# An attention program for two batches: written out in place of a loop of two turns

## The chip, the core and the metric

The kernel runs on one core of a Trainium2 chip. The core has five engines that run their own instruction streams side by side and meet at semaphores: TensorE (PE, matmuls and transposes), VectorE (DVE), ScalarE (ACT), GpSimd (POOL) and SyncE (SP, which here only issues DMAs). The metric is the device time in microseconds, the median of several executions.

## The reference

One transformer layer with adaptive layer norm, for two batches of 2048 tokens with 256 features. Attention has two query heads that share one key and one value head of 128; it is causal. The second half is a mixture of eight experts in which every expert is computed for every token and weighted by a thresholded gate.

```python
mod = (silu(c) @ wmod)                       # shifts, scales and gates, per batch
h = layernorm(x) * (1 + ca) + sa
k = rope(h @ Wk.T); v = h @ Wv.T; q = rope(einsum('btd,hkd->bhtk', h, Wq))
w = softmax(causal(q @ k.T * HS**-0.5)); o = w @ v
x = x + ga * (o @ Wo.T)
h = layernorm(x) * (1 + cb) + sb
gate = softmax(h @ Wg + bg); thr = sigmoid(h @ Wt + bt) * 0.125
g = where(gate >= thr, gate - thr, 0); g = g / sum(g)
x = x + gb * sum_e g_e * (gelu(h @ W1[e] + b1[e]) @ W2[e] + b2[e])
```

All in float32; products are made of three matmuls of split operands (hi*hi, hi*lo, lo*hi).

## The kernel before

The program has two blocks with a barrier of all engines between them: attention (up to about 503 us of the profile) and the mixture (the rest).

Attention handles the 4096 tokens as 2 batches of 16 tiles of 128. For each tile there are stages: `norm`, `rstd` and `xn` (layer-norm statistics, reciprocal root, normalized rows; three engines pass small tiles round), `normT` (transposition and modulation), `hT` and `qkv` (projection), `rope` and `rotT` (rotation, transposition of q and k), `S`, `M`, `N`, `E` (scores, row maximum, its negative, exponentials), `T` and `PV` (transposition of the weights, product with v), `O` and `Y` (output projection; its last instruction, L830, writes the tile's new rows `x1`), `gate`, `h2`, and, twice in a batch, `G1` and `G2` (gates of eight tiles; twelve small VectorE instructions, each of which waits for the one before). A planner with a cost for each stage writes one list `ORDER[engine]` for each engine, for one batch. Each engine works its list off strictly in order; stages of one batch never overlap those of the other.

Before the change each of PE, ACT, DVE and POOL runs its list inside a hardware loop of two turns, `Fori(0, B)`. So `b` is a register, and so is every semaphore value that depends on it: `done(...)` returns `b * total + count`, which is a register operation before the instruction or wait that uses it (REGISTER_ALU, ISA in the listings below). Addresses that depend on `b` are `bass.ds(...)`, also registers. Each engine closes a turn with `batch_end`, which waits until the whole batch is done (`act_h2`, `pool_h2`, `dve_G2`, `dve_x1`), and the loop's compare and branch. VectorE opens a turn with L720, the copy of the batch's modulation columns, and the first `norm`. SyncE has no such loop: its list was written out for both batches already, with constants.

The helper `wait_alone` waits for a value in an instruction of its own instead of attaching the wait to the engine instruction that follows.

Of the kernel before, what the change touches and what calls it, by code (L numbers as in the profile page):

```python
# [32 lines left out]
P = 128  # L33
B, T, D = 2, 2048, 256
# [3 lines left out]
NT = T // P  # L38
# [13 lines left out]
GT = NT // 2  # L52
# [193 lines left out]
def adaln_block(nc, x, wqkvT, woT, wgt, bgt, w1, b1, w2, b2, c, wmod, cos, sin, ident, mask, out):  # L246
# [5 lines left out]
    with outer:  # L252
# [6 lines left out]
        def keep(name, shape, dt=F32):  # L259
            return outer.enter_context(nc.sbuf_tensor(name, shape, dt))  # L260
# [8 lines left out]
        h2_hi = keep("h2_hi", [P, KD, TILES * P], F32R)  # L269
# [3 lines left out]
        gates = keep("gates", [P, TILES, E])  # L273
        out_gates = keep("out_gates", [P, B, 2 * D])
# [14 lines left out]
        s_batch = sem("s_batch")  # L289
# [41 lines left out]
        with attention:  # L331
# [19 lines left out]
            less_max, exps, weights = (sb(n, [P, GT, E]) for n in ("less_max", "exps", "weights"))  # L351
# [3 lines left out]
            mod_cols = sb("mod_cols", [P, B, 4, KD])  # L355
            mod_b = sb("mod_b", [P, 4, KD])
# [3 lines left out]
            hf = sb("hf", [P, 2, KD, P])  # L360
# [16 lines left out]
            def batch_end(eng, b):  # L377


                wait_alone(eng, (act_h2, b * NT + NT), (pool_h2, b * NT + NT),  # L380
                           (dve_G2, b * (NT // GT * G2_STEPS) + NT // GT * G2_STEPS),
                           (dve_x1, b * NT + NT))
# [60 lines left out]
            def _(pe):  # L443
# [29 lines left out]
                    if was:  # L473
                        pe.wait_ge(*done(dve_T if was[0] == "T" else act_hf, b, *was))

                with pe.Fori(0, B) as b:
                    for stage in ORDER["PE"]:
                        kind, t, g = stage
                        if kind == "S":
# [95 lines left out]
                        elif kind == "normT":  # L575
# [7 lines left out]
                                        last = nc.tensor.transpose(tr_ps[:, T_BANK[stage], c0:c0 + P],  # L583
                                                                   xn[:, i, k * P:(k + 1) * P], ident_sb[:])
                            last.then_inc(pe_normT, 1)
                    batch_end(pe, b)

            @block.scalar
            def _(act):
# [2 lines left out]
                nc.scalar.activation(c_exp[:], c_cols[:], ACT.Exp, scale=-1.0).then_inc(s_pre_a, 1)  # L592
                act.wait_ge(s_pre_e, 1)
                nc.scalar.activation(out_gates[:], score_ps[:, 0:B, :], ACT.Copy).then_inc(s_pre_a, 1)
                with act.Fori(0, B) as b:
                    for kind, t, g in ORDER["ACT"]:
                        if kind == "E":

# [45 lines left out]
                        elif kind == "norm":  # L644

                            act.wait_ge(*done(pool_var, b, "norm", t))
                            nc.scalar.activation(ln_v[:], var_eps[:], ACT.Ln).then_inc(act_ln, 1)
                            act.wait_ge(*done(act_ln, b, "norm", t))
                            nc.scalar.activation(rs0[:], ln_v[:], ACT.Exp, scale=-0.5).then_inc(act_rstd, 1)
                        elif kind == "rotT":  # L650

                            act.wait_ge(*done(pe_rotT, b, "rotT", t))
                            if ok(t - 2):
                                act.wait_ge(*done(pe_S, b, "S", t - 2, 4 + chunks_of(t - 2) - 1))
                            nc.scalar.activation(q_hi[:, t % 2, :], m_ps[:, 0:NH * P],
                                                 ACT.Copy).then_inc(act_rot, 1)
                            nc.scalar.activation(k_hi[:, t * P:(t + 1) * P], m_ps[:, NH * P:ROT],
                                                 ACT.Copy).then_inc(act_rot, 1)
                        elif kind == "normT":

                            act.wait_ge(*done(pe_normT, b, "normT", t))
                            if ok(t + 1):
                                act.wait_ge(*done(pool_hT, b, "hT", t + 1))
                            if ok(t - 4):
                                act.wait_ge(*done(pool_h2, b, "h2", t - 4))
                                act.wait_ge(*done(pe_gate, b, "gate", t - 4))
                            if t == -2:
                                act.wait_ge(s_batch, b + 1)
                            for i, tile in enumerate((t + 2, t - 3)):
                                if ok(tile):  # L670
                                    for k in range(KD):
                                        c0 = (i * KD + k) * P
                                        last = nc.scalar.activation(
                                            hf[:, i, k, :], tr_ps[:, T_BANK[kind, t, g], c0:c0 + P], ACT.Identity,
                                            scale=mod_b[:, 2 * i, k:k + 1], bias=mod_b[:, 2 * i + 1, k:k + 1])
                            last.then_inc(act_hf, 1)
                        elif kind == "G1":
                            act.wait_ge(*done(dve_G1, b, "G1", t, 0, G1_STEPS))
                            nc.scalar.activation(exps[:], less_max[:], ACT.Exp).then_inc(act_G1, 1)
                            nc.scalar.activation(exp_z[:], logits[:, t * GT:(t + 1) * GT, E], ACT.Exp,  # L680
                                                 scale=-1.0).then_inc(act_G1, 1)
                        elif kind == "h2":

                            wait_alone(act, done(act_hf, b, "normT", t + 3))
                            nc.scalar.activation(h2_hi[:, :, bass.ds(b * T + t * P, P)], hf[:, 1, :, :],
                                                 ACT.Copy).then_inc(act_h2, 1)
                    batch_end(act, b)

            @block.vector
            def _(dve):  # L690
# [24 lines left out]
                for s in s_st:  # L715
                    dve.sem_inc(s, 16)
                wide = lambda a: a[:].unsqueeze(2).broadcast_to([P, GT, E])
                with dve.Fori(0, B) as b:

                    nc.vector.tensor_copy(mod_b[:].unsqueeze(1), mod_cols[:, bass.ds(b, 1), :, :]).then_inc(s_batch, 1)  # L720
                    for kind, t, g in ORDER["DVE"]:
                        if kind == "M":

# [44 lines left out]
                        elif kind == "G2":  # L768
                            def step(ins, n):
# [17 lines left out]
                            step(nc.vector.scalar_tensor_tensor(row_b[:], row_a[:], 0.0, row_a[:],  # L787
                                                                ALU.is_equal, ALU.add), 10)
                            step(nc.vector.reciprocal(thr_b[:], row_b[:]), 11)
                            nc.vector.tensor_tensor(gates[:, bass.ds(b * NT + t * GT, GT), :], weights[:],  # L790
                                                    wide(thr_b), ALU.mult).then_inc(dve_G2, 1)
                        elif kind == "rope":

# [55 lines left out]
                        elif kind == "wo":  # L849
# [4 lines left out]
                                ins.then_inc(dve_wo, 1)  # L854
                                dve.wait_ge(*done(dve_wo, b, "wo", 0, 0, WO_STEPS, WO_STEPS - n))

                            raw = out_gates[:, bass.ds(b, 1), :]
                            size = wo_ga[:].rearrange("p h d -> p (h d)").unsqueeze(1)
                            dve.wait_ge(s_pre_a, 2)
                            dve.wait_ge(l_wo, 16)  # L860
# [9 lines left out]
                        elif kind == "xn":  # L870
# [8 lines left out]
                                last = nc.vector.tensor_scalar(xn[:, 1, :], x1_sb[:, t % 2, :], mv[:, 1, 0:1],  # L879
                                                               rstd[:, 1:2], ALU.subtract, ALU.mult)  # L880
                            last.then_inc(dve_xn, 1)
                    batch_end(dve, b)

            @block.gpsimd
            def _(pool):
# [3 lines left out]
                nc.gpsimd.tensor_tensor(wqkv_lo[:], wqkv_raw, wqkv_hi[:].bitcast(F32),  # L889
                                        ALU.subtract).then_inc(s_pre_p, 1)  # L890
                pool.wait_ge(s_pre_p, 2)
                with pool.Fori(0, B) as b:
                    for kind, t, g in ORDER["POOL"]:
                        if kind == "hT":

# [39 lines left out]
                        elif kind == "h2":  # L935

                            wait_alone(pool, done(act_h2, b, "h2", t))
                            tok = bass.ds(b * T + t * P, P)
                            nc.gpsimd.tensor_tensor(h2_lo[:, :, tok], hf[:, 1, :, :], h2_hi[:, :, tok].bitcast(F32),
                                                    ALU.subtract).then_inc(pool_h2, 1)  # L940
                    batch_end(pool, b)

            attention_block.close()

# [365 lines left out]
```

## Time and profile before

| what | value |
| --- | --- |
| median of 3 runs | 1945.32 us (1945.28, 1945.32, 1950.65) |
| profiled execution, its span | 1947.1 us |
| PE busy in the span | 1846.1 us (95%) |
| DVE / ACT / POOL busy | 52% / 53% / 30% |
| DVE: first turn starts (L720) | 17.91 us |
| DVE: second turn starts (L720) | 263.21 us |
| mixture: its first matmul | 507.52 us |

The profile gives no time of its own for the profiled execution besides its span; the span is 1.8 us longer than the median of the runs. Busy times and starts are those of this one execution. An engine's idle time is followed by the name of what released it; "issue" means that the profile shows no other instruction that it waited for.

### The profile page before, as it was taken

Reading aid. Unit: us, or ns where it says so; the run is one execution under the profiler, and the core shown is the slowest. Engines: PE = TensorE matmul, PEld = TensorE weight load, DVE = VectorE, ACT = ScalarE, POOL = GpSimd, SP = SyncE. Lnnn points to the kernel's source line nnn. Section 1 sums busy time; section 2 is a strip of 40 time slices with the busy share of each in tenths; the row PEclk is TensorE's granted clock in tenths of the full one; section 3 lists DMA queues with packets and bytes.
Section 4 is the critical chain, followed back from the end, with each engine's and each line's share of the span. In section 5 each row is a group of like instructions: output and inputs, shape, how many; then the busy total and the mean of one; then the engine's idle time right before and its main releaser. Section 6 shows DMA issues by size and latency. Waiting matters only on the chain. (4 is left out here: it accounts for less than half of the span.)

```text
span 1947.1 us, 35092 instructions
## 1 busy us (share of the span) xinstructions
PE 1846.1 (95%) x9856; PEld 1572.1 (81%) x9856; DVE 1016.1 (52%) x2054; ACT 1041.6 (53%) x2066; POOL 587.9 (30%) x873
## 2 busy tenths in 40 slices
PE   5899947999699999999999999999999999999998
PEld 4689936899588888888888888888888888888886
DVE  3799757997444444444444444444444444444555
ACT  2577726777455455554545554545455555545453
POOL 4433134331233222232222332222322223322344
PEclk7899959999799999999999999999999999999999
DMA  3000000001200000010001000000100010000111
GB/s 91 22 23 23 18 8 23 23 18 31 73 0 0 25 21 0 0 46 0 0 0 46 0 0 29 17 0 0 46 0 0 0 46 0 0 11 22 43 43 54
DMA packets 33155, 39.15 MB, mean 20 GB/s; under 512 B 6704, under 2 KB 29232, under 8 KB 33072
## 3 DMA queue, kind: packets, MB, share of 16 engines
q1 hardware_dynamic: 33072, 38.20, 6.2%
q8 instruction: 33, 0.54, 0.1%
q14 instruction: 50, 0.41, 0.1%
HBM read 29.80 MB, written 8.39 MB: 20 GB/s over the span
## 5 line engine op out<-in xcount | busy, mean ns | idle before, releaser
L1146 DVE TENSOR_TENSOR h_lo<-probs_even,h_hi 128x512 fp32r<-128x512 f32 x512 | 387.2, 756 | 725.0 <-ACT h_hi L1112 724.9
L1107 ACT ACTIVATE probs_even<-score_ps,b_cols 128x512 f32<-128x512 f32 x512 | 353.0, 689 | 701.3 <-issue 665.2
L1212 POOL TENSOR_TENSOR acc<-acc,probs_even 128x256 f32 (+1 forms) x256 | 229.3, 926 | 1016.3 <-ACT probs_even L1125 1016.3
L1057 PE MATMUL score_ps<-h_hi,w_hi 128*128 (+1 forms) x1024 | 405.8, 396 | 9.8 <-DVE w_lo L1187 9.8
L1057 PE MATMUL score_ps<-h_lo,w_hi 128*128 (+1 forms) x1024 | 405.8, 396 | 0.0
L1057 PE MATMUL score_ps<-h_hi,w_lo 128*128 (+1 forms) x1024 | 399.3, 390 | 0.0
L1071 PE MATMUL tr_ps<-w_both,h_hi 128*128 128x512 f32 x1024 | 376.4, 392 | 0.0
L1112 ACT ACTIVATE h_hi<-score_ps,b_cols 128x512 fp32r<-128x512 f32 x512 | 348.7, 681 | 0.0
L1074 PE MATMUL tr_ps<-w_both,h_lo 128*128 128x256 f32 x1024 | 286.0, 279 | 0.0
L1057 PEld LDWEIGHTS score_ps<-h_hi,w_hi 128*128 128x128 f32 x1024 | 193.0, 188 | 58.5 <-DVE w_lo L1187 9.9
L1057 PEld LDWEIGHTS score_ps<-h_hi,w_lo 128*128 128x128 f32 x1024 | 193.2, 189 | 44.9
L1071 PEld LDWEIGHTS tr_ps<-w_both,h_hi 128*128 128x128 f32 x1024 | 192.2, 188 | 42.3
L1057 PEld LDWEIGHTS score_ps<-h_lo,w_hi 128*128 128x128 f32 x1024 | 192.9, 188 | 21.1
L1074 PEld LDWEIGHTS tr_ps<-w_both,h_lo 128*128 128x128 f32 x1024 | 192.2, 188 | 19.9
L1071 PE MATMUL o_ps<-w_both,h_hi 128*128 128x512 f32 x512 | 206.3, 403 | 0.0
L1071 PE MATMUL m_ps<-w_both,h_hi 128*128 128x512 f32 x512 | 203.8, 398 | 0.0
L1159 DVE SCALAR_TENSOR_TENSOR acc<-b_rows,gates,acc 128x256 f32 (+1 forms) x256 | 163.5, 639 | 0.0
L1074 PE MATMUL o_ps<-w_both,h_lo 128*128 128x256 f32 x512 | 145.4, 284 | 0.0
L1074 PE MATMUL m_ps<-w_both,h_lo 128*128 128x256 f32 x512 | 142.1, 278 | 0.0
L1071 PEld LDWEIGHTS m_ps<-w_both,h_hi 128*128 128x128 f32 x512 | 96.3, 188 | 26.5
L1071 PEld LDWEIGHTS o_ps<-w_both,h_hi 128*128 128x128 f32 x512 | 96.3, 188 | 21.7
L620 ACT ACTIVATE pT_hi<-tr_ps 128x512 fp32r<-128x512 f32 (+1 forms) x144 | 82.5, 580 | 44.3 <-PE tr_ps L508 42.7
(146 smaller groups left out, 2688.1 us busy)
## 6 DMA issues: line engine op xcount, KB each, us to landing
w_raw<-w_dram SPq DMA_DIRECT2D x8, 1024.0 KB, 4.9
probs_even<-w_dram SPq DMA_DIRECT2D x8, 1024.0 KB, 7.4
x_sb<-x_dram SPq DMA_DIRECT2D x32, 128.0 KB, 2.2
x_scratch<-x_sb SPq DMA_DIRECT2D x32, 128.0 KB, 1.7
w_raw<-x_scratch SPq DMA_DIRECT2D x8, 512.0 KB, 4.5
out_dram<-acc SPq DMA_DIRECT2D x7, 512.0 KB, 3.2
probs_even<-wmod_dram SPq DMA_DIRECT2D x4, 256.0 KB, 3.5
b_rows<-b_dram SPq DMA_DIRECT2D x8, 128.0 KB, 2.9
```

The source lines that it names most:

```text
L620: nc.scalar.activation(pT_hi[:, slot, 0:n], tr_ps[:, T_BANK[kind, t, g], 0:n], ACT.Copy).then_inc(act_T, 1)
L1057: last = nc.tensor.matmul(up_ps[f % 4], w[par][:, k, f * P:(f + 1) * P], h[:, k, tok], start=(i == 0), stop=(i == 3 * KD - 1))
L1071: nc.tensor.matmul(down_ps[j], h_hi[:, f % 4, tok], w2_both[par][:, f, :, :].rearrange("p a d -> p (a d)"), start=(f == 0), stop=False)
L1074: last = nc.tensor.matmul(down_ps[j][:, 0:D], h_lo[:, f % 4, tok], w2_both[par][:, f, 0, :], start=False, stop=(f == FT - 1))
L1107: nc.scalar.activation(g_sb[:, f % 2, :], up_ps[f % 4], ACT.Gelu_apprx_tanh, bias=bias).then_inc(g_done, 1)
L1112: nc.scalar.activation(h_hi[:, f % 4, :], up_ps[f % 4], ACT.Gelu_apprx_tanh, bias=bias).then_inc(up_free, 1)
L1146: nc.vector.tensor_tensor(h_lo[:, f % 4, :], g_sb[:, f % 2, :], h_hi[:, f % 4, :].bitcast(F32), ALU.subtract).then_inc(lo_done, 1)
L1159: nc.vector.scalar_tensor_tensor(tile(j), b2_rows[:, par:par + 1, :], gate_of(e, t, j), tile(j), ALU.mult, ALU.add).then_inc(dve_bias, 1)
L1212: nc.gpsimd.tensor_tensor(tile(j), tile(j), y_sb[:, j - 2:j - 1, n * D:(n + 1) * D], ALU.add).then_inc(sem_, 1)
```

## The change

On PE, ACT, DVE and POOL the hardware loop becomes a Python loop, so the list of stages is emitted twice, once with b = 0 and once with b = 1. All semaphore values and addresses in it become constants. `batch_end` is no longer called. The order of the stages on each engine and within a batch stays as it was, and no data instruction is added or left out.

```diff
-                with pe.Fori(0, B) as b:
+                for b in range(B):
                     for stage in ORDER["PE"]:
...
-                    batch_end(pe, b)
...
-                with act.Fori(0, B) as b:
+                for b in range(B):
...
-                            nc.scalar.activation(h2_hi[:, :, bass.ds(b * T + t * P, P)], hf[:, 1, :, :],
+                            nc.scalar.activation(h2_hi[:, :, slice(b * T + t * P, b * T + (t + 1) * P)], hf[:, 1, :, :],
...
-                    batch_end(act, b)
...
-                with dve.Fori(0, B) as b:
-
-                    nc.vector.tensor_copy(mod_b[:].unsqueeze(1), mod_cols[:, bass.ds(b, 1), :, :]).then_inc(s_batch, 1)
+                for b in range(B):
+
+                    nc.vector.tensor_copy(mod_b[:].unsqueeze(1), mod_cols[:, b:b + 1, :, :]).then_inc(s_batch, 1)
...
-                            nc.vector.tensor_tensor(gates[:, bass.ds(b * NT + t * GT, GT), :], weights[:],
+                            nc.vector.tensor_tensor(gates[:, b * NT + t * GT:b * NT + (t + 1) * GT, :], weights[:],
...
-                            raw = out_gates[:, bass.ds(b, 1), :]
+                            raw = out_gates[:, b:b + 1, :]
...
-                    batch_end(dve, b)
...
-                with pool.Fori(0, B) as b:
+                for b in range(B):
...
-                            tok = bass.ds(b * T + t * P, P)
+                            tok = slice(b * T + t * P, b * T + (t + 1) * P)
...
-                    batch_end(pool, b)
```

The places below are on VectorE. First, the end of a turn before the change: the last instructions of `G2`, `batch_end` (the row that waits for five semaphores), the branch back, and behind it what follows the second turn.

```order
806 L789 RECIPROCAL thr_b<-row_b 128x8 [waits dve_G2]
807 L772 REGISTER_ALU
808 L790 ISA [waits dve_G2]
809 L790 TENSOR_TENSOR gates<-weights,thr_b 128x64
810 L325 REGISTER_ALU
811 L718 REGISTER_ALU [waits dve_G2,pool_h2,dve_x1,act_h2,s_ld0]
812 L718 COMPARE_AND_BRANCH
813 L943 UNCONDITIONAL_BRANCH
814 L1137 UNCONDITIONAL_BRANCH [waits barrier_Pool_Activation_PE_DVE_SP_release]
```

The same place of the changed kernel, between the first batch and the second (its lines are numbered a little lower).

```order
474 L787 RECIPROCAL thr_b<-row_b 128x8 [waits dve_G2]
475 L788 TENSOR_TENSOR gates<-weights,thr_b 128x64 [waits dve_G2]
476 L718 COPY mod_b<-mod_cols 128x8
477 L837 BN_STATS stats<-x_sb 128x6 [waits s_x0]
478 L845 BN_AGGR mv<-stats 128x2 [waits dve_stats,s_ld0]
479 L874 TENSOR_SCALAR xn<-x_sb,mv,rstd 128x256 [waits pool_ln]
```

The register instructions, the wait for the batch and the branch are gone, and the copy that opens the next batch stands directly behind the last gate instruction, with no wait.

Second, the entry of VectorE into its first turn, before the change: the branch into the loop waits for the setup.

```order
11 L718 UNCONDITIONAL_BRANCH [waits s_pre_d]
12 L718 ISA
13 L720 COPY mod_b<-mod_cols 128x8
14 L838 ISA
15 L839 BN_STATS stats<-x_sb 128x6 [waits s_x0]
```

And in the changed kernel, behind the last setup instruction.

```order
10 L712 CAST mask_r<-mask_raw 128x128 [waits s_ld7,s_pre_d]
11 L718 COPY mod_b<-mod_cols 128x8 [waits s_pre_d]
12 L837 BN_STATS stats<-x_sb 128x6 [waits s_x0]
13 L845 BN_AGGR mv<-stats 128x2 [waits dve_stats,s_ld0]
14 L874 TENSOR_SCALAR xn<-x_sb,mv,rstd 128x256 [waits pool_ln]
```

Two register instructions and the branch are gone; the order of the data instructions is the same.

## Rows read from the trace of the kernel before

**Rows 1.** The page's head and busy times (busy us, share, instructions).

```profile
span 1947.1 us, 35092 instructions
...
PE 1846.1 (95%) x9856; PEld 1572.1 (81%) x9856; DVE 1016.1 (52%) x2054; ACT 1041.6 (53%) x2066; POOL 587.9 (30%) x873
```

**Rows 2.** Stretches of both turns: length, busy PE, PEld, DVE, ACT, POOL; PEclk, DMA, GB/s.

```profile
17.91:55.63 37.72, 20.12 (x78) 14.96 (x78) 20.64 (x55) 15.23 (x50) 19.35 (x42) 0.67 0.02 3
55.63:65.54 9.91, 7.74 (x33) 6.29 (x34) 6.16 (x21) 3.38 (x12) 2.79 (x7) 0.66 0.09 26
...
75.38:248.03 172.65, 164.96 (x1151) 149.51 (x1149) 146.40 (x377) 126.35 (x360) 54.33 (x119) 0.99 0.07 21
263.21:301.22 38.01, 21.94 (x78) 16.12 (x78) 20.70 (x55) 15.23 (x50) 19.33 (x42) 0.58 0.01 2
301.22:309.02 7.80, 5.36 (x34) 4.59 (x35) 6.61 (x20) 3.64 (x12) 3.07 (x7) 1.00 0.11 34
...
318.58:491.20 172.62, 164.93 (x1151) 149.65 (x1149) 146.44 (x378) 126.25 (x360) 54.31 (x119) 0.99 0.10 30
```

**Rows 3.** Busy times by stretch, the mixture.

```profile
600.00:1900.00 1300.00, 1300.00 (x6533) 1095.65 (x6532) 571.86 (x935) 658.71 (x1051) 368.00 (x454) 1.00 0.04 15
```

**Rows 4.** Waits of VectorE, 258 to 265 us (total, times, longest).

```profile
DVE mod_b L720 <- issue: 4.1, 1, 4.1
```

**Rows 5.** Timeline between the turns (start, duration, ..., [idle before <- releaser]).

```profile
254.23 0.72 POOL L939 TENSOR_TENSOR h_lo<-hf,h_hi 128x256 f32 x1 [2.88 <-ACT h_hi L685]
...
254.96 0.15 DVE L755 TENSOR_TENSOR logits<-o_ps,bgt_sb 128x9 f32<-128x9 f32 x1
255.23 0.22 DVE L764 TENSOR_REDUCE row_a<-logits 128x8 f32<-128x64 f32 x1
...
258.51 0.20 DVE L789 RECIPROCAL thr_b<-row_b 128x8 f32<-128x8 f32 x1
258.86 0.22 DVE L790 TENSOR_TENSOR gates<-weights,thr_b 128x64 f32 x1
263.21 0.17 DVE L720 COPY mod_b<-mod_cols 128x8 f32 x1 [4.12 <-issue]
```

**Rows 6.** DMA queues, 258 to 265 us, then 700 to 1500 us (packets, MB, share).

```profile
q14 instruction: 6, 0.05, 2.1%
q8 instruction: 2, 0.03, 2.1%
...
q14 instruction: 2, 0.02, 0.0%
```

**Rows 7.** Timeline of VectorE at its entry into the first turn.

```profile
17.25 0.23 DVE L714 CAST mask_r<-mask_raw 128x128 fp32r<-128x128 f32 x1
17.91 0.17 DVE L720 COPY mod_b<-mod_cols 128x8 f32 x1 [0.43 <-DVE mask_r L714]
```

**Rows 8.** Timeline of VectorE early in the second turn.

```profile
280.96 0.15 DVE L733 TENSOR_REDUCE top<-top 128x1 f32<-128x1 f32 x1
281.15 0.15 DVE L735 TENSOR_SCALAR neg<-top 128x1 f32<-128x1 f32 x1
281.55 0.43 DVE L839 BATCH_NORM_STATS2 stats<-x_sb 128x6 f32<-128x256 f32 x1 [0.25 <-issue]
...
300.59 0.48 DVE L822 SCALAR_TENSOR_TENSOR y_sb<-m_ps,rsums,x_sb 128x256 f32<-128x256 f32 x1
301.22 0.48 DVE L830 SCALAR_TENSOR_TENSOR x_sb<-m_ps,rsums,y_sb 128x256 f32<-128x256 f32 x1
```

**Rows 9.** Timeline of PE in the full part of the first turn.

```profile
163.76 0.28 PE L527 MATMUL o_ps<-pT_hi,v_lo 128*128 128x256 f32 x1
163.88 0.60 PE L508 MATMUL tr_ps<-ident_sb,probs_even 128*128 128x128 f32 x4
```

**Rows 10.** Timeline where the attention block ends.

```profile
502.03 0.22 DVE L790 TENSOR_TENSOR gates<-weights,thr_b 128x64 f32 x1
...
503.23 1.91 ACT L1130 ACTIVATE w_hi<-w_raw 128x2048 fp32r<-128x2048 f32 x1 [3.96 <-PEq L943]
```

## The prediction, on record before the changed kernel ran

> **What bounds the kernel now.** I read the page first. PE is busy for 95% of the span [rows 1], so time can only come out of PE's idle stretches, or out of work that delays PE. The busy times by stretch come next. In the mixture PE is busy for 1300.00 of 1300 us at the full clock [rows 3]; the change leaves that half alone, and nothing is to be had there. In attention the same view, cut where the two turns begin and where tiles 0, 1, 2 and 15 finish, shows three kinds of stretch [rows 2]. From tile 2 to tile 15 PE is busy 164.96 of 172.65 us in one turn and 164.93 of 172.62 in the other: PE is the bound, and the two turns agree to 0.03 us. From a turn's start to its first finished tile, 38 us long, no engine is busy for more than 22: a chain of small steps over DVE, POOL, ACT and PE sets the time. And between the turns, from 248.03 to 263.21, PE has almost nothing to do. There and in the ramp behind it the reader is to look for single waits on the chain. The waits of VectorE between 258 and 265 us have one entry, 4.1 us before L720, released by "issue" [rows 4]. That is the change's place.
>
> **The jump between the turns.** The last instruction of the first turn on DVE, L790, starts at 258.86 and takes 0.22, so it ends at 259.08; L720 starts at 263.21 [rows 5]. In the changed program L720 stands directly behind L790 and has no wait. A copy that waits for nothing can start at the end of the instruction before it or, as the two overlap in the pipeline, a little earlier; I take 259.0. The gain is 263.21 - 259.0 = 4.2 us. Does it reach the end? What follows L720 on DVE is the statistics of tile 0, then POOL, ACT, POOL, DVE and PE in turn, each idle until its predecessor in that chain; the input rows of the batch's first tiles were loaded long ago by SP, whose program did not change. DVE's queue is in order, so the chain can't start before 259.0 either: the gates of the last eight tiles stand ahead of it. What is late next is thus DVE's own G2 chain, and 4.2 is both the value and nearly the upper end. The lower end is what would remain if part of the gap were a real wait.
>
> What is the gap made of? The wait for the batch is not it: the last piece of work on another engine, POOL's h_lo, ended at 254.23 + 0.72 = 254.95, 4.1 us before DVE got there [rows 5]. In the window 258 to 265 the only DMA traffic is instructions, 6 and 2 packets with 0.08 MB [rows 6], while the program is being re-entered at its head. At the other end of the loop, where the branch is not taken, the whole way from the end of L790 (502.03 + 0.22 = 502.25) through the loop's end and the barrier of all engines to ACT's first instruction takes 503.23 - 502.25 = 0.98 us [rows 10]. So over 3 us of the 4.1 belong to jumping back and loading code again.
>
> The Trainium skill (Advanced Engine Details and Errata, Control Flow Timing) gives a compare-and-branch about 108 ns. By that figure alone the loop's branch would be a fortieth of the gap, and if the rest were a wait that survives, the change would bring 0.1 us here instead of 4.2. The row of 4.1 us with its instruction packets speaks against reading the figure as the price of this jump.
>
> **The entry of the first turn.** DVE's L714 ends at 17.25 + 0.23 = 17.48 and L720 starts at 17.91, a gap of 0.43 [rows 7]. The wait for L714 and two semaphore increments stay, the branch and a register instruction go. A plain dependent instruction on DVE starts 0.04 after the end of its predecessor (280.96 + 0.15 = 281.11, next at 281.15) [rows 8]. I leave 0.15 for wait and increments: gain 0.28, between 0 and 0.39. It lies on the chain, as nothing else starts the first turn.
>
> **The register instructions.** They cost nothing where they can run ahead: between L733 and L735 (281.15) there is one and the gap is 0.04. They cost where the instruction in front of them waits: ahead of L839 at 281.55 a register instruction carries the wait, and the gap is 281.55 - 281.30 = 0.25 instead of 0.04; ahead of L830 at 301.22 it is 301.22 - 301.07 = 0.15 [rows 8]. In the tail of a turn the gap before L764 is 255.23 - 255.11 = 0.12 and that before L790 258.86 - 258.71 = 0.15 [rows 5]; each would be 0.04. The tail is a pure DVE chain, so 0.08 + 0.11 count in full, and the first G2's L790 has a like gap of which I take half: 0.25 a turn, 0.5 for both. In the ramp I count 0.21 for L839 and 0.1 for L830 and a few tenths of such hops on ACT and POOL, of which about half are on the chain: 0.3 a turn, 0.6 for both. The bounds for these two together are 0.2 (only the tail's second L790 counts) and 3 (all 16 waits of this kind in DVE's list of a turn, at 0.1, count in half, and the other engines bring as much).
>
> On PE (201 a turn in the built program) I count nothing. In the full part the transposes of L508 have register instructions and a wait in front of them and still start 163.88 - 163.76 = 0.12 us after the last matmul's start, while that matmul, 0.28 long, is under way [rows 9]. The cover is PE's own queue of matmuls; if it were gone, 60 such groups a turn at 0.05 would be 3 us a turn, which is the upper end of another case below.
>
> **The exit.** Of the 0.98 us behind the second turn [rows 10] the rest of batch_end, the compare and the branch go, the barrier stays. I take 0.25, between 0 and 0.5. Mixture work behind it (weight splits on ACT and DVE, then PE) follows in a fixed chain and moves as a whole.
>
> **PE's clock.** This is the term that the trace can't fix. In tile 1 of the first turn the granted clock was 0.66 and the tile took 9.91 us; in the second turn it was 1.00 and the tile took 7.80 [rows 2]. Before tile 0 it was 0.67 against 0.58, and there the second turn was 0.29 longer (38.01 against 37.72). So the same work costs up to 2.1 us more when the clock is at its lower level (1.2 GHz in place of 2.4) at the wrong moment. The second ramp moves by some 5 us in time, PE's idle stretch before it gets 4 us shorter, and the moments at which the clock steps need not move along. The second turn had the better draw in tile 1, so the change is likelier to lose here than to win: I take -0.3, with bounds -2.1 and +0.5.
>
> **Sum.** 4.2 + 0.28 + 0.5 + 0.6 + 0.25 - 0.3 = 5.5 us. The profiled execution had a span of 1947.1; it becomes 1941.6. The median of the runs was 1945.32, 1.8 below the span; the same gain gives 1939.8 us.
>
> **Rivals.**
> - *The clock turns against the second ramp.* Tile 1, or the stretch before it, runs at the lower level as in the first turn. For it: the draw of the first turn. Against: a shorter idle stretch in front. Full price 2.1 in place of 0.3: 1939.8 + 1.8 = 1941.6. Chance 0.20.
> - *Waits and registers were worth more.* The waits of small tiles on all engines get quicker, or PE's queue did feel the register instructions. For it: over 700 register instructions a turn go on the four engines together, counted in the built program. Against: the 0.04 us and 0.12 us gaps above. With 2 us more: 1937.8. Chance 0.13.
> - *The change doesn't do what it says.* The code between the batches still has to be loaded, as it was at the loop's head, and most of the 4.1 us stays. For it: the packets of rows 6. Against: the first turn ran the same list straight from memory with no such gap anywhere in it. If 4 of the 4.2 stay: 1943.8. Chance 0.07.
> - *Slower.* The attention code changes length, so the mixture's loops lie elsewhere in memory. If ACT's or DVE's outer loop over pairs of experts no longer stays loaded, each jump back costs the 4.1 us of rows 4. There are three pairs, so two jumps back, 8.2 us if nothing covers them: 1939.8 + 8.2 = 1948.0. It decides from two uncovered jumps on; with one the kernel is still not slower. Against: between 700 and 1500 us queue 14 loaded 2 packets [rows 6], and PE had no idle time at all [rows 3]. Chance 0.04.
>
> The Trainium skill (Runtime: NRT & Kernel Launch, Instruction fetch mechanics) says that an engine holds only two blocks of 256 instructions and that a taken branch outside them must fetch its target. By that rule the last rival depends on where a loop of about 260 instructions falls across block borders, and no run before this one shows that.
>
> **How the numbers follow.** The forecast has the remaining 0.56. Three cases (forecast, clock, registers) reach from 1937.8 to 1941.6; with the spread of their terms, and the part of the third rival that lies below 1943, the range is 1937.0 to 1942.8, and the rest beyond it is under 2 in 10. A measurement of this kernel can tell about 0.3%, 5.8 us, from no change, and my gain of 5.5 lies just under that line. Of the forecast's 0.56 I put 0.31 beyond the line (gains of 5.8 to 6.8) and 0.25 short of it; with the second rival's 0.13 faster gets 0.44. The clock, the third rival and the forecast's rest give 0.52 for within 0.3%. Slower has 0.04.
>
> **What would show it.** In the changed profile L718 on DVE (the copy) follows the last gate instruction within 0.1 us and the entry "issue 4.1" is gone; if a gap over 1 us remains there, the first step is wrong. PE's last idle stretch before the second batch shrinks by 4 us. The stretch from tile 2 to tile 15 stays at 172.6 us in both batches; if it shrinks by more than 0.5, the register instructions did cost PE something. From the copy to the finished tile 0 it takes 37.2 to 38 us in the second batch, and tile 1 takes 7.8 us at a clock of 1.00; with 9 to 10 at a lower clock the first rival holds. The gaps before L839, L830, L764 and L790 shrink to 0.04. From the first matmul of the mixture to the end it stays 1439.6 us (1947.1 - 507.5, the mixture's first matmul in the table of the profile). Anything else there would point to the last rival.

## The result and the profile after

The changed kernel takes 1938.08 us in the median of 4 runs (1936.33 to 1939.7), the kernel before 1946.65 (1945.28 to 1950.65, 4 runs): a ratio of 0.995 [0.9937, 0.9963], faster (in brackets the 95% interval). The same pair measured once more, on one chip, gave 1939.49 us (5 runs) against 1946.73 (29 runs), 0.9965 [0.9952, 0.9978]. The forecast was 1939.8 us. Its time lay close; that the gain would more likely be too small to be told from no change was wrong. The intervals are 0.13% wide to either side, 2.5 us, so the line of 0.3% that the forecast drew was too coarse as well: a gain of 5.5 us would have been clear of it by this measurement.

The page of the profile after, its head and its busy times as in [rows 1]; this execution took 1937.46 us.

```profile
span 1935.3 us, 33653 instructions
...
PE 1842.7 (95%) x9856; PEld 1571.8 (81%) x9856; DVE 1016.2 (53%) x2054; ACT 1043.7 (54%) x2066; POOL 589.6 (30%) x873
```

The same work in 11.8 us less, with 1439 fewer register and branch instructions. Next VectorE's timeline at the boundary of the batches, to be held against [rows 5].

```profile
254.91 0.17 DVE L785 SCALAR_TENSOR_TENSOR row_b<-row_a 128x8 f32<-128x8 f32 x1
255.11 0.20 DVE L787 RECIPROCAL thr_b<-row_b 128x8 f32<-128x8 f32 x1
255.35 0.22 DVE L788 TENSOR_TENSOR gates<-weights,thr_b 128x64 f32<-128x64 f32 x1
255.49 0.17 DVE L718 COPY mod_b<-mod_cols 128x8 f32<-128x8 f32 x1
255.56 0.42 DVE L837 BATCH_NORM_STATS2 stats<-x_sb 128x6 f32<-128x256 f32 x1
```

The last gate instruction ends at 255.57 and the copy starts at 255.49, 0.08 before: the idle time of 4.12 is gone in full, and no instruction packet moves between 250 and 258 us. The gap ahead of L788 is 0.04 (0.15 before). Now busy times by stretch, cut as in [rows 2] (columns as there; PEclk, the clock granted to PE, is 1.00 for 2.4 GHz and 0.50 for 1.2 GHz), and the mixture.

```profile
15.91:54.53 38.62, 21.30 (x77) 16.32 (x78) 20.55 (x54) 15.24 (x50) 19.25 (x42) 0.68 0.06 13
54.53:63.61 9.08, 7.38 (x35) 6.09 (x35) 6.20 (x20) 3.38 (x12) 2.81 (x7) 0.70 0.10 29
73.38:244.89 171.51, 164.85 (x1151) 149.82 (x1150) 145.31 (x377) 126.80 (x360) 54.36 (x119) 0.99 0.07 21
255.49:294.32 38.83, 23.22 (x77) 17.48 (x78) 20.55 (x55) 15.19 (x50) 19.27 (x42) 0.54 0.00 1
294.32:303.10 8.78, 6.35 (x38) 4.94 (x37) 7.51 (x21) 3.90 (x13) 3.48 (x8) 0.94 0.10 30
312.60:484.17 171.57, 164.91 (x1152) 149.81 (x1150) 145.28 (x377) 126.70 (x360) 54.36 (x119) 0.99 0.09 30
600.00:1900.00 1300.00, 1300.00 (x6549) 1097.38 (x6548) 576.08 (x936) 661.05 (x1052) 369.59 (x449) 1.00 0.05 16
```

From tile 2 to tile 15 each batch is 1.1 us shorter, with PE busy for as many microseconds as before. The second ramp with its tile 1 is longer, 47.61 against 45.81 us, at a granted clock of 0.54 and 0.94 where it was 0.58 and 1.00. In the mixture 1300 us hold 16 matmul records more (6549 against 6533): it ran 0.24% faster. Last the end of attention, as in [rows 10].

```profile
494.63 0.22 DVE L788 TENSOR_TENSOR gates<-weights,thr_b 128x64 f32<-128x64 f32 x1
...
495.29 1.91 ACT L1126 ACTIVATE w_hi<-w_raw 128x2048 fp32r<-128x2048 f32 x1 [3.30 <-PEq L939]
...
499.58 0.79 PE L1053 MATMUL score_ps<-h_hi,w_hi 128*128 128x512 f32 x1 [8.90 <-DVE w_lo L1183]
```

ACT follows the gates after 495.29 - 494.85 = 0.44 us (0.98 before).

With such cuts the whole execution can be taken apart: start of the first copy, ramp (copy to tile 0), tiles 1 and 2, tiles 2 to 15, tail (tile 15 to the last gate's end), jump (to the next copy), exit (to PE's first matmul of the mixture), mixture. The last two columns are one pair of executions on one chip (e1 is the kernel before again, e2 the changed one again).

| part, us | before | after | gain | e1 | e2 | gain |
|---|---|---|---|---|---|---|
| start | 17.91 | 15.91 | 2.00 | 17.67 | 17.25 | 0.42 |
| batch 0: ramp, tiles 1, 2 | 57.47 | 57.47 | 0 | 54.79 | 54.87 | -0.08 |
| tiles 2 to 15 | 172.65 | 171.51 | 1.14 | 172.63 | 171.53 | 1.10 |
| tail | 11.05 | 10.68 | 0.37 | 11.07 | 10.67 | 0.40 |
| jump | 4.13 | -0.08 | 4.21 | 4.16 | -0.08 | 4.24 |
| batch 1: ramp, tiles 1, 2 | 55.37 | 57.11 | -1.74 | 54.94 | 57.38 | -2.44 |
| tiles 2 to 15 | 172.62 | 171.57 | 1.05 | 172.43 | 171.65 | 0.78 |
| tail | 11.05 | 10.68 | 0.37 | 11.07 | 10.66 | 0.41 |
| exit | 5.27 | 4.73 | 0.54 | 5.17 | 4.73 | 0.44 |
| mixture | 1439.58 | 1435.72 | 3.86 | 1439.47 | 1439.14 | 0.33 |
| sum (span) | 1947.1 | 1935.3 | 11.8 | 1943.4 | 1937.8 | 5.6 |

Two gains of the first pair do not recur in the second: 3.86 us in the mixture, and most of the 2.00 in the setup. The other parts agree to 0.3 us, but for the second ramp, which loses 0.7 us more in the second pair.

### The profile page after: what moved, and what is told of

It is laid out like the page before. It is cut to its first block and busy times, and to the rows that moved or that the text cites. A ratio compares the mean times of both kernels' runs of the same rounds, so it can differ in the third digit from the quotient of the medians.

```text
span 1935.3 us, 33653 instructions
## 1 busy us (share of the span) xinstructions
PE 1842.7 (95%) x9856; PEld 1571.8 (81%) x9856; DVE 1016.2 (53%) x2054; ACT 1043.7 (54%) x2066; POOL 589.6 (30%) x873
## 5 line engine op out<-in xcount | busy, mean ns | idle before, releaser
L1053 PE MATMUL score_ps<-h_hi,w_hi 128*128 (+1 forms) x1024 | 399.3, 390 | 8.9 <-DVE w_lo L1183 8.9
L1053 PE MATMUL score_ps<-h_hi,w_lo 128*128 (+1 forms) x1024 | 407.4, 398 | 0.0
L1067 PE MATMUL o_ps<-w_both,h_hi 128*128 128x512 f32 x512 | 200.2, 391 | 0.0
```

The costliest lines, as they stand in the source:

```text
L1053: last = nc.tensor.matmul(up_ps[f % 4], w[par][:, k, f * P:(f + 1) * P], h[:, k, tok], start=(i == 0), stop=(i == 3 * KD - 1))
L1067: nc.tensor.matmul(down_ps[j], h_hi[:, f % 4, tok], w2_both[par][:, f, :, :].rearrange("p a d -> p (a d)"), start=(f == 0), stop=False)
```

## The experiments

**e1 and e2, the two kernels again.** No edit.

> The kernel before, unchanged, timed against itself. The trace after the change showed 178.34 us for each expert before and 177.91 after (time between the loads of two experts' weights on SP), though nothing of the mixture was changed. Theory A (that was a difference between two executions or chips): here the ratio to the kernel before is 1.000, and the time per expert of this trace lies anywhere between 177.9 and 178.4, the same as in the other traces of this call. Theory B (the mixture's rate hangs on where its code lies in memory): 178.3 here, as in the trace of before, and 177.9 in the written-out kernel of the same call. Both: 4.1 us of idle time before L720 on DVE, tiles 2 to 15 in 172.6 us.

> The changed kernel, unchanged, on the same chip as the kernel before, for a closer ratio. Theory A: gain over the kernel before of 6 to 8 us: 4.2 for the jump, 0.5 for the exit, 0.2 for the entry, 0.4 for each tail, 1.1 a batch for tiles 2 to 15, minus or plus the clock; time per expert as in e1. Theory B: 3.5 us more than that, 9.5 to 11 us, with 177.9 us per expert against 178.3 in e1.

e1 against the kernel before: 1.0005 [0.9996, 1.0014]; e2: 0.9965 [0.9952, 0.9978]. The mixture can be read off SyncE's loads of an expert pair's biases: after, before, then e2 and e1 (start, duration).

```profile
675.94 0.34 SPq L1021 DMA_DIRECT2D b_rows<-b_dram  x1
853.86 0.35 SPq L1021 DMA_DIRECT2D b_rows<-b_dram  x1
```
```profile
684.72 0.35 SPq L1025 DMA_DIRECT2D b_rows<-b_dram  x1
863.07 0.35 SPq L1025 DMA_DIRECT2D b_rows<-b_dram  x1
```
```profile
675.44 0.35 SPq L1021 DMA_DIRECT2D b_rows<-b_dram  x1
853.79 0.35 SPq L1021 DMA_DIRECT2D b_rows<-b_dram  x1
```
```profile
681.02 0.35 SPq L1025 DMA_DIRECT2D b_rows<-b_dram  x1
859.36 0.35 SPq L1025 DMA_DIRECT2D b_rows<-b_dram  x1
```

177.92 us after, 178.35 before, and again 178.35 and 178.34 in e2 and e1. The same changed code takes either time, so theory A holds, and the 3.9 us belong to the execution or its chip and not to the change. Which of the two is open.

**e3, the loop without batch_end.** Only the call at the end of each engine's turn goes:

```
-                    batch_end(pe, b)        # and the same for act, dve, pool
```

> The kernel before with its loop of two turns and its register values, but without the wait at the end of a turn on all four engines. Theory 1 (the gap between the turns is the jump back and the loading of code): 3.5 to 4.1 us of idle time before L720 stay, the time is that of the kernel before to 0.5 us. Rival (the gap is the wait of batch_end and its register work): the gap falls below 1 us and 3 to 4 us of the gain appear.

Measured 1944.57 us, 0.9984 [0.9975, 0.9994]. VectorE's timeline at the boundary:

```profile
258.85 0.23 DVE L788 TENSOR_TENSOR gates<-weights,thr_b 128x64 f32 x1
261.92 0.17 DVE L718 COPY mod_b<-mod_cols 128x8 f32 x1 [2.84 <-issue]
```

The loop without its wait still stands for 2.84 us, with 6 and 2 instruction packets between 250 and 265 us, as many as in [rows 6]; its tiles 2 to 15 take 172.62 and 172.68 us, its tails 11.07 and 11.06, as before. The exit is 4.73, as after. So batch_end was worth 4.16 - 2.84 = 1.3 us at the jump and 0.44 at the exit, and nothing elsewhere: 1.8 by parts, 3.1 [1.2, 4.9] by the ratio. That is more than I had expected of the wait, whose releasers had all been done for 4 us, and the 2.84 us left are less than the 3.5 to 4.1 that I had expected of the jump.

**e4, written out with batch_end.** The other half alone:

```
                 for b in range(B):
                     ...
+                    batch_end(pe, b)        # and the same for act, dve, pool
```

> The changed kernel, written out for both batches, with the wait at the end of a batch put back on all four engines. Theory 1 (the gap was the jump): the wait finds everything done on DVE, the gap before the second batch's copy is 0.2 to 0.5 us in place of 0.04, and the time is within 1 us of the changed kernel. Rival (the gap was the wait): 3 to 4 us of idle time come back, and the time goes back by that much.

Measured 1941.85 us, 0.998 [0.9971, 0.9988]. The boundary, then ACT's waits from 860 to 870 us (total, times, longest) with PE's:

```profile
253.48 0.22 DVE L790 TENSOR_TENSOR gates<-weights,thr_b 128x64 f32<-128x64 f32 x1
253.93 0.17 DVE L720 COPY mod_b<-mod_cols 128x8 f32<-128x8 f32 x1 [0.23 <-DVE gates L790]
```
```profile
ACT probs_even L1107 <- issue: 4.5, 1, 4.5
PEld tr_ps L1071 <- DVE h_lo L1146: 1.2, 1, 1.2
PE tr_ps L1071 <- DVE h_lo L1146: 0.8, 1, 0.8
```

In straight code batch_end costs 0.23 + 0.08 = 0.3 us at the boundary and 5.18 - 4.73 = 0.45 at the exit. That is less at the boundary than the 1.3 of e3, so the parts of the gap don't add. Where the other 1.0 us comes from was not tested. It can be the register work that the wait needs in the loop. Or it is that `batch_end` lets all four engines jump at the same moment: 5 instruction packets of all engines fall into VectorE's gap before the change (259.08 to 263.21 us; 4 in e1), and 1 into its gap in e3 (259.08 to 261.92), where the other engines had jumped earlier. The second fence shows something else. In two of the eight experts ACT stops for 4.5 and 5.0 us, 4 packets of instructions arrive each time, and PE loses 0.8 and 1.3 us; these experts take 179.43 and 179.93 us instead of 178.35, together 2.66. By medians e4 is 2.4 us slower than e2, where I had expected less than 1. That is the prediction's slower rival, the mixture's outer loop loading code again at its turns, met in a kernel that differs from the changed one by 22 instructions. The changed kernel escapes it: in e2 PE is busy for all of 690 to 1410 us.

**e5 to e8, one engine back in its loop.** The changed kernel, with the loop on PE, DVE, ACT or POOL alone (on DVE, ACT and POOL the addresses made from b too):

```
-                for b in range(B):
+                with dve.Fori(0, B) as b:
```

> The changed kernel, but PE keeps its hardware loop with 201 register instructions a turn; ACT, DVE and POOL stay written out, and there is no wait at the end of a turn. Read from the trace, not from the time. Tiles 2 to 15 took 172.6 us a batch in the kernel before and 171.5 to 171.65 in the changed one; the tail behind tile 15 took 11.05 to 11.07 and 10.67. Theory P (PE's own register instructions cost the 1.0 us): tiles 2 to 15 go back to 172.4 to 172.6 in both batches, the tail stays 10.67. Theory D (DVE's did, in waits that PE has for DVE): they stay at 171.6. PE's jump back lies in its idle time: no gap before DVE's second copy, and the second ramp within 38.5 +- 1.

> The changed kernel, but DVE keeps its hardware loop with its 277 register instructions a turn, without the wait at the end of a turn; the others are written out. Theory P: tiles 2 to 15 stay at 171.6, the tail goes back to 11.05 (its DVE chain is the tail). Theory D: tiles 2 to 15 go back to 172.6. Both: a jump of 2.8 us between the turns on DVE, as in the looped kernel without the wait (2.84).

> The changed kernel, but ACT keeps its hardware loop with 153 register instructions a turn, the others are written out. Theories P and D: tiles 2 to 15 stay at 171.6 and the tail at 10.67. A third theory, A (ACT's registers lie between PE and DVE in the chain of weights): 172.6 here. No gap on DVE between the batches, since ACT's jump has 8 us of idle time to hide in.

> The changed kernel, but POOL keeps its hardware loop with 98 register instructions a turn, the others are written out. Read from the trace. POOL was idle for 70% of the span; its register instructions run ahead in that time. Theory: tiles 2 to 15 stay at 171.5 to 171.65 a batch, the tail at 10.67 to 10.8, no gap between the batches on DVE. Rival (POOL's registers lie in the chain of the layer norm, five steps of which are POOL's): tiles 2 to 15 over 172 and the ramp over 39 us at the same clocks.

| us | e2, none | PE | DVE | ACT | POOL | e1, all and batch_end |
|---|---|---|---|---|---|---|
| jump on DVE | -0.08 | -0.08 | 2.91 | -0.09 | -0.08 | 4.16 |
| tiles 2 to 15, batch 0 | 171.53 | 172.16 | 172.30 | 169.95 | 171.98 | 172.63 |
| batch 1 | 171.65 | 171.96 | 172.53 | 171.53 | 172.18 | 172.43 |
| tail, batch 1 | 10.66 | 10.66 | 10.90 | 10.77 | 10.77 | 11.07 |
| run | 1940.0 | 1939.21 | 1946.84 | 1936.93 | 1937.54 | 1945.21 |

Each of e5 to e9 was run once, so its trace is read and not its time. Only DVE's loop brings the jump back; the others jump too, while DVE finishes its gates. (169.95 is a matter of the clock, see the end.) Between tile 2 and tile 15 PE, DVE and POOL each bring back 0.3 to 0.9 us of the 1.1 and 0.8, ACT nothing. Neither theory P nor theory D holds alone, and for POOL I had expected none. Where these sit shows in the stretches from tile 2 to 5, 5 to 8 and 8 to 15 of batch 1, e1 and then e2 (first column length, second busy PE, third from the end the granted clock).

```profile
315.26:351.88 36.62, 31.60 (x203) 27.67 (x201) 31.61 (x88) 25.02 (x75) 14.94 (x31) 0.95 0.08 23
351.88:388.96 37.08, 36.33 (x249) 32.28 (x248) 33.97 (x90) 29.44 (x87) 14.98 (x30) 1.00 0.08 23
388.96:487.69 98.73, 96.79 (x704) 89.52 (x702) 80.87 (x201) 71.98 (x200) 24.57 (x58) 1.00 0.11 35
```
```profile
311.62:347.81 36.19, 31.84 (x203) 28.03 (x203) 31.10 (x87) 25.27 (x75) 15.02 (x31) 0.95 0.07 23
347.81:384.26 36.45, 36.13 (x247) 32.17 (x247) 33.61 (x90) 29.31 (x87) 14.66 (x30) 1.00 0.07 23
384.26:483.27 99.01, 97.02 (x704) 89.58 (x703) 80.59 (x201) 72.02 (x200) 24.49 (x58) 1.00 0.10 35
```

The gain is 0.43 and 0.63 us up to tile 8 and -0.28 behind it. These parts are of two kinds.

From tile 5 to 8 the clock is 1.00, and PE's idle time falls from 0.75 to 0.32 us. One of its waits has a name in e1's list for that stretch; in e2's list there is none.

```profile
PE tr_ps L583 <- DVE xn L879: 0.7, 3, 0.2
```

The same stretch in e5 (PE in its loop), e6 (DVE) and e8 (POOL):

```profile
346.91:383.63 36.72, 36.18 (x248) 32.16 (x247) 33.72 (x90) 29.32 (x87) 14.67 (x30) 1.00 0.07 23
354.68:391.49 36.81, 36.22 (x248) 32.28 (x248) 33.85 (x90) 29.47 (x88) 14.97 (x30) 1.00 0.08 23
345.30:381.70 36.40, 36.10 (x247) 32.15 (x247) 33.58 (x90) 29.30 (x87) 14.66 (x30) 1.00 0.08 23
```

PE's registers cost 36.72 - 36.45 = 0.27 us here and DVE's 0.36, and the two add up to the whole 0.63; ACT's (36.45) and POOL's cost nothing. Batch 0 gives the same: 0.30, 0.37, and 0.66 for all.

The gain up to tile 5 lies all in one tile, the stretch from tile 2 to 3, in which the granted clock is 0.85 or 0.86 (1.00 in the 9.62):

| us | e2, none | PE | DVE | ACT | POOL | e1, all |
|---|---|---|---|---|---|---|
| tile 2 to 3, batch 0 | 11.21 | 11.75 | 11.59 | 9.62 | 11.63 | 11.80 |
| batch 1 | 11.19 | 11.49 | 11.81 | 11.21 | 11.77 | 11.60 |

Here PE is idle for 2.2 to 2.8 us, PE's, DVE's or POOL's loop alone brings most of the loss back, and the three do not add. Of the twelve batches of written-out kernels with this clock eleven take 11.14 to 11.21 us. But batch 1 of e10 below, where no engine has register values, takes 11.73. So this part can be lost without them: that they set it is likely and not shown, and POOL's share rests on it alone.

**e9, a small loop at the boundary.** The changed kernel, with four empty turns of a loop on DVE ahead of the second copy; its code is a handful of instructions:

```
+                    if b == 1:
+                        with dve.Fori(0, 4):
+                            dve.sem_inc(spare, 1)
```

> The changed kernel with a small hardware loop of 4 turns put on DVE between the two batches; its body is one semaphore increment that nobody waits for. So there are 3 jumps back, to code that was just run. Theory 1 (the 2.8 us of a jump between the turns are the loading of the code it jumps to): the gap before the second copy is 0.3 to 1.2 us in all, some 0.1 to 0.3 a turn. Rival (a taken branch itself costs that much on DVE): 3 times 2.8, 8.4 us.

```profile
252.82 0.22 DVE L792 TENSOR_TENSOR gates<-weights,thr_b 128x64 f32<-128x64 f32 x1
254.34 0.17 DVE L722 COPY mod_b<-mod_cols 128x8 f32<-128x8 f32 x1 [1.29 <-issue]
```

Four turns with three jumps back and all their registers take 1.30 us together, with the overlap of 0.08 that is gone 1.38 or about 0.35 a turn, a little over what I had expected at most. No instruction packet moves between 252 and 262 us. One jump to the head of a long list takes 2.8 to 2.9 (e3, e6), with packets. The difference of about 2.5 us is thus for code that has to be loaded again. The Trainium skill (Advanced Engine Details and Errata, Control Flow Timing) gives about 108 ns for a compare-and-branch. A small loop's turn here, with its semaphore and registers, comes to three times that, and the long jump to 26 times. By the Trainium skill (Runtime: NRT & Kernel Launch, Instruction fetch mechanics) a taken branch out of the loaded blocks must wait until its target is fetched. e3 and e6 (gap with packets) and e9 (no packets, no such gap) agree with that.

**e10, waits on the instruction itself.** The changed kernel, five waits of attention (ACT's h2, DVE's aggregate, three of POOL's) attached to the instruction that needs them instead of standing alone (one of the five is shown):

```
-                            wait_alone(pool, made(2))
+                            pool.wait_ge(*made(2))
```

> The changed kernel with the five separate waits of the attention stages (h2 on ACT and POOL, the layer norm's aggregation on DVE, variance and third step of the root on POOL) made ordinary waits, which can be attached to the instruction. Waits of their own put 0.10 us before the aggregation on DVE and 0.16 before the POOL step, where an attached one puts 0.04 and 0.08. Theory S (a separate wait costs 0.06 to 0.08 us on the chain): each round of the layer norm, from statistics to normalized rows, goes from 2.78 us to 2.55, four of them stand in each ramp and two in each tail, gain 1 to 2 us in all, less where the clock draws otherwise. Rival: these gaps are there anyway (write-back of small results), gain 0.

Measured 1934.8 us, 0.9936 [0.9923, 0.9948]. The hops in question at the start, first e2, then e10:

```profile
19.29 0.19 POOL L925 TENSOR_TENSOR rs<-rs,var_eps 128x2 f32<-128x2 f32 x1
19.64 0.19 POOL L927 TENSOR_SCALAR rs<-rs 128x2 f32<-128x2 f32 x1 [0.16 <-POOL rs L925]
```
```profile
18.42 0.20 POOL L925 TENSOR_TENSOR rs<-rs,var_eps 128x2 f32<-128x2 f32 x1
18.70 0.19 POOL L927 TENSOR_SCALAR rs<-rs 128x2 f32<-128x2 f32 x1
```

A wait that stands alone costs 0.08 us here (0.16 to 0.08), and 0.07 ahead of the aggregate (0.11 to 0.04). The first round of the layer norm, from statistics to normalized rows, takes 2.66 us in place of 2.83. Tails fall from 10.67 to 10.33 and the ramps with tile 1 to 44.86 and 44.50 us. In e9, where the later part of both ramps ran at the same clocks (0.86, then 1.00), the ramps took 45.16 and 45.43 and the tails 10.75 and 10.68. So the parts give 0.3 + 0.9 + 0.8 = 2.0 us, the upper end of what was expected; 0.5 of it is lost again in batch 1's tile 2 to 3. Against e2, measured on another chip, it is 4.7 us by medians; in the profiles 3.1 of it lie in the second ramp, which e2 ran at a lower clock (47.63 us, 0.70 in tile 1). Each has its ratio to the kernel before: the intervals of e10 and e2 don't touch, while that of the first measurement of the changed kernel overlaps e10's. So the hops are shown, and the size of the whole only roughly.

**e11, batch 1's first norms ahead of the last gates.** With no turn between the batches their lists can be interleaved. The first three norm stages of batch 1 stand before the gate chains that end batch 0; mod_cols is read in place of its copy:

```
+EARLY = {
+    "DVE": {("xn", 17, 0): [("norm", -3, 0)], ("G2", 0, 0): [("xn", -3, 0), ("norm", -2, 0)],
+            ("G1", 1, 0): [("xn", -2, 0), ("norm", -1, 0)]},
+    "ACT": {("G1", 0, 0): [("norm", -3, 0)], ("h2", 15, 0): [("norm", -2, 0)]},
+    "POOL": {("rstd", 17, 0): [("norm", -3, 0), ("rstd", -3, 0)]},
...
-                for b in range(B):
-                    for kind, t, g in ORDER["DVE"]:
+                for b, part in parts("DVE"):
+                    for kind, t, g in part:
```

> The changed kernel with the first layer-norm stages of batch 1 put ahead of batch 0's last gate chains on DVE, ACT and POOL, and the modulation columns read in place instead of through a copy. The forecast said that DVE's gate chain is what is late next once the jump is gone; this takes it off the path. Theory 1: normalized rows of batch 1's first three tiles come 3 to 6 us earlier, and the whole kernel is 4 to 6 us faster than the changed kernel, minus or plus 2 for the clock. Rival (the ramp's start isn't what sets its end; PE and ACT are): under 1.5 us.

Measured 1931.6 us, 0.9916 [0.9901, 0.9931].

```profile
252.98 0.40 DVE L896 TENSOR_SCALAR xn<-x_sb,mv,rstd 128x256 f32<-128x256 f32 x1
...
256.19 0.41 DVE L896 TENSOR_SCALAR xn<-x_sb,mv,rstd 128x256 f32<-128x256 f32 x1 [1.50 <-POOL rstd L953]
...
259.84 0.23 DVE L810 TENSOR_TENSOR gates<-weights,thr_b 128x64 f32<-128x64 f32 x1
259.99 0.41 DVE L896 TENSOR_SCALAR xn<-x_sb,mv,rstd 128x256 f32<-128x256 f32 x1
```

The first three normed tiles of batch 1 (L896) start at 252.98, 256.19 and 259.99; in the profile after they start at 258.34, 261.56 and 265.26. The idle hops of one chain are filled by the other. Does it reach the end of the ramp? From tile 15 of batch 0 to tile 2 of batch 1 it takes 59.67 us here, and 65.95 and 66.10 in e7 and e8, which have the old order and nearly the same mean clock (0.69, here 0.71); in e2 it takes 67.97. So the gain is 6.3 to 6.4 us, and the rival fell. Neither 6.3 nor the 7.9 us between the medians of e11 and e2, from two chips, is a ratio measured side by side.

**e13, e10 and e11 together.** Both edits.

> Both of the two edits before (ordinary waits in the attention stages; batch 1's first layer-norm stages ahead of batch 0's last gate chains). If both theories hold the gains add: 5 to 8 us faster than the changed kernel, 12 to 15 faster than the kernel before.

Measured 1929.12 us, 0.9909 [0.9897, 0.9922], span 1926.3: the fastest of all, 9 us below the changed kernel and 17.4 below the kernel before of the same measurement, more than the 12 to 15 expected. Its interval overlaps that of e11, and from tile 15 to the next tile 2 it takes 60.11 us, not less than e11, so what e10's edit adds on top of e11 isn't settled.

## Why the prediction was wrong, step by step

- *The jump* (4.2): 4.21 and 4.24. Right. What it was made of was nearly right: "over 3 us" were to be jumping back and loading code, and without batch_end 2.84 us stay (2.9 with the overlap of 0.08), about 2.5 of them code loading (e3, e6, e9); batch_end was worth 1.3, more than the 0.98 of the way out [rows 10] had let it be. The third rival, that the code is loaded anyway, fell: there is no packet at the boundary.
- *The entry* (0.28): L712 to L718 has a gap of 0.26 where it was 0.43, so 0.17.
- *The tails* (0.5 for both): 0.74 and 0.81. A size. e6 gives DVE's own registers 0.23 a tail, e7 and e8 0.1 each to ACT and POOL, which I had left out there.
- *The ramps* (0.6 for both): the hops are there. From the copy to the second row maximum of a batch (L727 before, L725 after) it took 25.83 and 25.80 us before, 25.28 and 25.36 after: 1.0 for both, in e1 and e2 0.6. Of it 0.40 a batch is fixed: the way from the first row maximum to the second takes 8.38 us with DVE in its loop (e6 too) and 7.98 without. But nothing of it arrived. Where the later part ran at like clocks (0.86, then 1.00), copy to tile 1 took 45.24 and 45.40 us in e1 and 45.37 in e2's batch 0: from the second row maximum to tile 0 the looped kernel took 11.89 and 11.82 us, and the written-out one 12.20 (12.11 and 12.26 in e9).
- *PE's registers* (0), and with them every hop between tile 2 and tile 15: **the step that failed.** "The stretch from tile 2 to tile 15 stays at 172.6 us in both batches" was false by 1.1 and 1.1, in e2 by 1.1 and 0.8: 2 us of gain where I had none. The row on which it rested [rows 9] lies in the full part, and there it holds: behind tile 8 e2 gained nothing (it lost 0.16 and 0.28). But I had taken 172.6 us with 164.9 busy for one full stretch; up to tile 8 it is not full. From tile 5 to 8 PE's registers cost 0.3 us and DVE's 0.4 in each batch, where I had counted nothing for either (e5, e6). Another 0.4 to 0.7 of a batch come from tile 2 to 3, and of these it is not shown that the registers set them. That was the second rival, at 2 us more: 1937.8, and 0.13 was too little for it.
- *The exit* (0.25): 0.54 and 0.44. A size, and in the first pair just above the bound of 0.5; e3 and e4 show that it is batch_end's wait.
- *The clock* (-0.3, bounds -2.1 and +0.5): the first rival held as well, in both profiles of the changed kernel. Batch 1's ramp with tiles 1 and 2 was 1.74 and 2.44 us longer, the latter beyond my bound. It is no fixed price of the change: e9's batch 1 runs the same list in 45.43 us from copy to tile 1, e2's in 47.63.
- *The mixture* (0, or slower): no jump back cost anything in the changed kernel; the 3.86 us faster of the profile after did not recur. e4 shows that the mechanism of the slower rival is real, at 2.7 us for two jumps and not 8.2, as PE's queue covers most of each.

Sum without the clock and what did not recur, from e1 and e2: 4.24 + 0.17 + 0.81 + 1.88 + 0.44 = 7.5 us against 5.8 forecast without the clock's -0.3. The 5.5 lay 0.3 under the line of 0.3%, so a miss of 2 us in one term was enough to turn the likelier case.

That the forecast came within 2 us of the time is partly luck. Between e1 and e2 the spans differ by 5.6 us, the forecast's gain almost exactly, but only because the 1.9 us that I had missed between tiles 2 and 15 and the 2.44 us that the second ramp lost stand against each other. And the base was 1945.32 us, 1.3 below the kernel's later median of 1946.65. Against the forecast, on the other hand, stands that the changed kernel's times are 2.2 us above their spans where the kernel before had 1.8, so 0.4 us of the gain in span don't arrive in the time.

## What to carry to other kernels

A jump back to the head of a long instruction list costs some 2.5 us more than one within a few instructions, each time it lies on the chain; where the turns are few, write them out, and then interleave their ends, which here was worth 6.3 us by the traces, more again than the jump. Cut a stretch that reads 95% busy once more before calling it full: the missing 5% can sit in a part where hops count. And hold each part of a gain against a second execution of the same pair, since here nearly half of the first profile's gain (3.86 + 1.83 of 11.8 us) was not the change's.

## What was not expected of the hardware

The time of identical code moves with the granted clock. From tile 2 to tile 15 of batch 0, e2 (171.53 us at a clock just under 1.00) and e7, whose stretch follows (length, busy, then the clock third from the end):

```profile
72.38:242.33 169.95, 163.26 (x1151) 148.40 (x1150) 145.04 (x377) 126.66 (x360) 54.32 (x119) 1.00 0.07 22
```

With the clock at 1.00 (2.4 GHz) throughout it takes 1.6 us less: e2 has a dip in it, by which tile 2 to 3 runs at 0.85 and takes 11.21 us in place of 9.62. e4 has the same 169.95. From a batch's copy to tile 1 the changed list took between 45.2 (e9, batch 0) and 47.7 us (after, batch 0), and no run here fixes the moments at which the clock moves. Why the shorter hops of the ramp did not arrive at tile 0, though the clock read 0.86 with and without them, is open.
